# Another order of all five engines' work in the turns of a gated delta rule kernel

## The reference, cut to what matters

```python
q, k = l2norm(conv(q)) * 64 ** -0.5, l2norm(conv(k))      # causal convolutions of 4 taps; v = conv(v)
def step(S, xs):
    q_t, k_t, v_t, g_t, b_t = xs
    S = S * exp(g_t)
    kv = k_t @ S
    delta = (v_t - kv) * b_t
    S = S + outer(k_t, delta)
    return S, q_t @ S
o = o * rsqrt(mean(o * o) + EPS) * norm_weight * sigmoid(z)
return o.reshape(B, S, 2048) @ w_out.T
```

## Time and profile before

| | |
|---|---|
| median of 3 runs (lowest, highest) | 3103.07 us (3101.98, 3112.64) |
| the profiled execution, its own time | 3102.21 us |
| its span, first to last instruction | 3100.4 us |
| mean granted clock of TensorE in it | 0.98 |
| TensorE's instructions | 42816 matmuls, 42816 weight loads |
| busy share: PE, DVE, ACT, POOL | 93%, 79%, 57%, 36% |

### The profile page before, as it was taken

How to read it: one execution, slowest core, us unless ns; L and a number is a source line. 1 busy time by engine, 2 the same in 40 slices (tenths; PEclk the granted TensorE clock), 3 DMA queues, 4 the chain that set the end, 5 groups by cost and what they waited for, 6 DMA issues and landing times. The chain is left out here.

```text
span 3100.4 us, 101425 instructions
## 1 busy us (share of the span) xinstructions
PE 2889.3 (93%) x42816; PEld 1955.3 (63%) x42816; DVE 2436.7 (79%) x5610; ACT 1753.3 (57%) x3242; POOL 1103.5 (36%) x904
## 2 busy tenths in 40 slices
PE   6699999999999999999999999999999999789998
PEld 3366666666666666666666666666666666645555
DVE  7688888888887888888888888888788888645654
ACT  6456666666665655666666566656566666333432
POOL 1444444334444444444434344444444444100000
PEclk9899999999999999999999999999999999899999
DMA  5455555454545444554555545544454545300000
GB/s 154 80 85 97 83 83 84 75 97 82 84 81 98 79 79 78 98 84 77 83 97 84 82 78 101 84 80 78 73 103 74 82 83 83 76 17 25 28 21 14
DMA packets 1298099, 241.85 MB, mean 78 GB/s; under 512 B 1248240, under 2 KB 1269104, under 8 KB 1296496
## 3 DMA queue, kind: packets, MB, share of 16 engines
q1 hardware_dynamic: 1297648, 235.36, 44.0%
HBM read 120.13 MB, written 39.58 MB: 52 GB/s over the span
## 5 line engine op out<-in xcount | busy, mean ns | idle before, releaser
L1342 PE MATMUL bank<-xT,w_sb 128*128 128x512 f32 x2048 | 980.5, 612 | 9.7 <-PEq L516 5.2
L784 POOL TENSOR_TENSOR kq<-kq,product 128x510 f32<-128x510 f32 (+2 forms) x384 | 449.2, 1183 | 717.4 <-ACT kq L873 707.4
L1342 PEld LDWEIGHTS bank<-xT,w_sb 128*128 128x128 f32 x2048 | 372.5, 192 | 374.5 <-issue 346.9
L772 POOL TENSOR_TENSOR dec_ap<-gcrow,gcb 128x1024 f32<-128x1024 f32 x64 | 121.9, 1904 | 653.7 <-DMA gcb<-gcb_d 653.7
L1088 DVE SCALAR_TENSOR_TENSOR kq<-bank,cw,kq 128x510 f32<-128x510 f32 (+2 forms) x384 | 285.8, 745 | 54.8 <-ACT kq L873 45.2
L1088 DVE SCALAR_TENSOR_TENSOR v_c<-bank,cw,v_c 128x510 f32<-128x510 f32 (+2 forms) x384 | 285.8, 744 | 15.9 <-ACT v_c L873 6.9
L1353 PE MATMUL bank<-kq 64*64 64x128 f32 x4096 | 277.6, 273 | 20.3 <-POOL kq L784 8.3
L940 ACT COPY delta<-bank 128x256 f32<-128x256 f32 x256 | 95.3, 372 | 343.7 <-PE bank L1410 343.5
L1457 PE MATMUL bank<-wo,u_sq 128*128 128x256 f32 x1024 | 260.5, 398 | 4.2 <-DVE u_sq L1180 3.5
L879 ACT ACTIVATE product<-bank,cw 128x512 f32<-128x512 f32 x384 | 249.2, 684 | 6.8 <-PE bank L1342 2.8
L1147 DVE TENSOR_TENSOR ap_mat<-bank,dec_ap 128x512 f32<-128x512 f32 x256 | 160.1, 684 | 115.9 <-PE bank L1435 108.9
(11 more groups left out here) (168 smaller groups left out, 5456.1 us busy)
## 6 DMA issues: line engine op xcount, KB each, us to landing
xT<-xT_d SPq DMA_DIRECT2D x64, 512.0 KB, 4.0
gcrow<-gcrow_d SPq DMA_DIRECT2D x128, 256.0 KB, 4.5
k_r<-k_tok SPq DMA_DIRECT2D x512, 64.0 KB, 2.3
v_r<-k_tok SPq DMA_DIRECT2D x512, 64.0 KB
a_d<-ap_mat SPq DMA_DIRECT2D x256, 64.0 KB
z_t<-z_d SPq DMA_DIRECT2D x256, 64.0 KB, 2.5
w_sb<-in_w_qkvz SPq DMA_DIRECT2D x8, 1024.0 KB, 6.8
x_un<-eye_un SPq DMA_DIRECT2D x64, 128.0 KB, 3.9
```

Source lines behind the costliest of these rows:

```text
L784: nc.gpsimd.tensor_tensor(t[:, :, d:SEQ], t[:, :, d:SEQ], prod[:, :, 0:SEQ - d], ALU.add).then_inc(tap_added[i], 1)
L1342: ins = nc.tensor.matmul(bank[:, :], w_two[m.grp % 2][:, h, s * P:(s + 1) * P], xT[:, h, :], start=(h == 0), stop=(h == HT - 1))
```

## The change

The order of work within a turn is changed on all engines; no product, transfer or vector instruction is added or removed. Some banks of the ring change their place with it, and so do the waits that protect them. Below are the turns as they are after it, shortened: lines with + are placed anew, the others are kept from the kernel before, whose own order is printed above. Indents are shortened. New semaphores: `mag_done`, `score_full[0]`, `tap_prod[3]` and `[4]`, `mats_done[1]` and `[2]`; gone: `acc_done`, `mats_done[0]`.

SyncE (only the step numbers fall by one; the order of the transfers stays):

```diff
...
 if s[4]:
+    wait_for(sp, mats_done[3], s[4], 1)
+    units_out(s[4])
...
+if s[3]:
+    wait_for(sp, kx_done[1], s[3], 1)
+    k_turned(s[3])
 if s[4]:
+    wait_for(sp, zt_done, s[4], 1)
+    z_out(s[4])
+    x_out(s[4])
...
```

GpSimd:

```diff
...
+if s[5]:
+    wait_for(pool, tap_added[0], s[5], 1)
+    add_tap(s[5], 0, 2)
+    wait_for(pool, tap_prod[3], s[5], 1)
+    add_tap(s[5], 1, 1)
...
+    wait_for(pool, tap_prod[5], s[5], 1)
+    add_tap(s[5], 1, 3)
+    wait_for(pool, cols_done, s[5], 1)
+    scale_decays(s[5])
+    wait_for(pool, egrow_done, s[5], 1)
+    end_decays(s[5])
+    clamp(s[5], 1)
...
+    scale_q(s[5], 1)
+    scale_q(s[5], 0)
 if s[4]:
+    wait_for(pool, gc_in, s[4], 48)
+    differences(s[4])
+    wait_for(pool, z_exp[0], s[4], 1)
+    clamp(s[4], 0)
     wait_for(pool, decay_done, s[4], 1)
     mask(s[4])
+    add_tap(s[4], 0, 1)
```

ScalarE:

```diff
...
 if s[4]:
     wait_for(act, comb_done[1], s[4], 1)
     gates(s[4], 1)
+if s[1]:
+    wait_for(act, proj_full[1], s[1], 1)
+    first_tap(s[1], 1, ring(s[1], 0))
 if s[4]:
     wait_for(act, comb_done[0], s[4], 1)
     gates(s[4], 0)
+if s[3]:
+    wait_for(act, zoff_full, s[3], 1)
+    outer_out(s[3])
+if s[2]:
+    log_z(s[2], 0)
...
+if s[3]:
+    wait_for(act, zr_full[0], s[3], 1)
+    delta_out(s[3], 0)
+    square_q(s[3])
...
     wait_for(act, diff_done, s[1], 1)
     magnitudes(s[1])
...
+    wait_for(act, proj_full[6], s[1], 1)
+    wait_for(act, z_log[0], s[1], 1, back=1)
+    exp_z(s[1], 0, ring(s[1], 1))
 if s[3]:
     wait_for(act, zr_full[1], s[3], 1)
     delta_out(s[3], 1)
 if s[2]:
     wait_for(act, sub_done[14], s[2], 1)
     turn_units(s[2])
 if s[1]:
+    wait_for(act, mag_done, s[1], 1)
+    decays(s[1])
+    wait_for(act, proj_full[5], s[1], 1)
+    first_tap(s[1], 5, ring(s[1], 1))
+    wait_for(act, proj_full[7], s[1], 1)
+    exp_z(s[1], 1, ring(s[1], 2))
+    first_tap(s[1], 3, ring(s[1], 3))
+    tap_product(s[1], 1, 1, ring(s[1], 3))
+    wait_for(act, tap_added[0], s[1], 1)
+    tap_product(s[1], 1, 2, ring(s[1], 3))
...
+if s[3]:
+    wait_for(act, zr_full[2], s[3], 1)
+    delta_out(s[3], 2)
...
+    wait_for(act, k_f_in, s[1], 128)
+    squares(s[1])
+    wait_for(act, tap_added[1], s[1], 1)
+    tap_product(s[1], 1, 3, ring(s[1], 3))
     wait_for(act, proj_full[4], s[1], 1)
     first_tap(s[1], 4, ring(s[1], 0))
     wait_for(act, sumk_done, s[1], 1)
     norms(s[1])
+    row_decays(s[1])
...
 if s[3]:
+    wait_for(act, zr_full[3], s[3], 1)
+    delta_out(s[3], 3)
     wait_for(act, o_full[3], s[3], 1)
     square_o(s[3], 1)
     square_o(s[3], 0)
     outer16_out(s[2])
 if s[3]:
     wait_for(act, ss_full[1], s[3], 1)
+    log_var(s[3], 1, ring(s[3], 0))
+    wait_for(act, ss_full[0], s[3], 1)
+    log_var(s[3], 0, ring(s[3], 3))
 if s[0]:
     wait_for(act, proj_full[0], s[0], 1)
+    first_tap(s[0], 0, ring(s[0], 3))
 if s[2]:
     wait_for(act, p1_full, s[2], 1)
     inner_out(s[2])
+if s[1]:
+    wait_for(act, z_clamped[1], s[1], 1)
+    wait_for(act, comb_done[1], s[1], 1, back=2)
+    log_z(s[1], 1)
...
```

VectorE:

```diff
...
 if s[2]:
+    sub_rest(s[2], 10)
+    sub_product(s[2], 11)
...
+    sub_product(s[2], 14)
+    sub_rest(s[2], 14)
 if s[1]:
     wait_for(dve, gc_in, s[1], 48)
     tail(s[1])
+if s[4]:
+    wait_for(dve, op_full[0], s[4], 1)
+    accumulate(s[4], 0, ring(s[4], 2))
+if s[3]:
+    decay_state(s[3], 1)
...
+if s[3]:
+    wait_for(dve, st_full[1], s[3], 1)
+    wait_for(dve, sdec_done[1], s[3], 1)
+    new_state(s[3], 1)
+    wait_for(dve, ks_full[2], s[3], 1)
+    residual(s[3], 2)
+if s[1]:
+    wait_for(dve, tap_done[5], s[1], 1)
+    conv(s[1], 5, ring(s[1], 1))
...
+if s[3]:
+    wait_for(dve, st_full[2], s[3], 1)
+    wait_for(dve, sdec_done[2], s[3], 1)
+    new_state(s[3], 2)
+    wait_for(dve, ks_full[3], s[3], 1)
+    residual(s[3], 3)
+if s[1]:
+    wait_for(dve, rk_done, s[1], 1)
+    wait_for(dve, rhs_done[3], s[1], 1, back=2)
+    columns(s[1])
+    conv(s[1], 4, ring(s[1], 0))
+    wait_for(dve, score_full[0], s[1], 1)
+    wait_for(dve, deca_done, s[1], 1)
+    wait_for(dve, o_full[3], s[1], 1, back=2)
+    matrices(s[1], 0, ring(s[1], 3))
+    wait_for(dve, score_full[1], s[1], 1)
+    matrices(s[1], 1, ring(s[1], 1))
+    wait_for(dve, score_full[2], s[1], 1)
+    matrices(s[1], 2, ring(s[1], 2))
+    wait_for(dve, score_full[3], s[1], 1)
+    matrices(s[1], 3, ring(s[1], 0))
+    turn_v(s[1], 1)
+if s[3]:
+    wait_for(dve, usq_done[1], s[3], 1)
+    add_squares(s[3], 1)
+    wait_for(dve, usq_done[0], s[3], 1)
+    add_squares(s[3], 0)
+if s[1]:
+    turn_v(s[1], 0)
+if s[2]:
+    wait_for(dve, z16_done, s[2], 1)
+    turn_back(s[2])
+if s[1]:
+    scale_k(s[1])
+if s[3]:
+    wait_for(dve, var_log[1], s[3], 1)
+    combine(s[3], 1, ring(s[3], 0))
+if s[0]:
+    wait_for(dve, tap_done[0], s[0], 1)
+    conv(s[0], 0, ring(s[0], 3))
+if s[3]:
+    wait_for(dve, var_log[0], s[3], 1)
+    combine(s[3], 0, ring(s[3], 3))
+    wait_for(dve, gate_done[1], s[3], 1)
+    gated(s[3], 1)
+    wait_for(dve, gate_done[0], s[3], 1)
+    gated(s[3], 0)
+if s[1]:
+    wait_for(dve, x_un_in, s[1], 16)
+    wait_for(dve, a_un_in, s[1], 16)
+    sub_product(s[1], 0)
+    sub_rest(s[1], 0)
+    sub_product(s[1], 1)
+if s[0]:
+    wait_for(dve, tap_done[1], s[0], 1)
+    conv(s[0], 1, ring(s[0], 0))
+if s[1]:
+    sub_rest(s[1], 1)
+    sub_product(s[1], 2)
+    sub_rest(s[1], 2)
+    sub_product(s[1], 3)
+    sub_rest(s[1], 3)
+if s[2]:
+    wait_for(dve, st_full[0], s[2], 1)
+    new_state(s[2], 0)
+if s[1]:
+    sub_product(s[1], 4)
+    sub_rest(s[1], 4)
+    sub_product(s[1], 5)
+    sub_rest(s[1], 5)
+if s[0]:
+    wait_for(dve, conv_done[0], s[0], 1)
+    wait_for(dve, v_f_in, s[0], 128, back=1)
+    turn_k(s[0], 0)
+if s[1]:
+    sub_product(s[1], 6)
+if s[0]:
+    wait_for(dve, conv_done[1], s[0], 1)
+    turn_k(s[0], 1)
+if s[1]:
+    sub_rest(s[1], 6)
+    sub_product(s[1], 7)
+    sub_rest(s[1], 7)
+    sub_product(s[1], 8)
+    sub_rest(s[1], 8)
+if s[2]:
+    wait_for(dve, ks_full[1], s[2], 1)
+    residual(s[2], 1)
+if s[1]:
+    sub_product(s[1], 9)
+    sub_rest(s[1], 9)
+    sub_product(s[1], 10)
...
```

TensorE:

```diff
...
+if s[3]:
+    wait_for(pe, qg_done[0], s[3], 1)
+    wait_for(pe, og_done[0], s[3], 1, back=1)
+    output(s[3], 0)
+    wait_for(pe, state_done[0], s[3], 1)
+    key_state(s[3], 1)
+if s[1]:
+    wait_for(pe, conv_done[0], s[1], 1)
+    project(s[1], 3, ring(s[1], 3))
+    wait_for(pe, z_exp[0], s[1], 1)
+    project(s[1], 5, ring(s[1], 1))
+if s[4]:
+    wait_for(pe, og_done[0], s[4], 1)
+    project_out(s[4], 0, ring(s[4], 2))
+if s[3]:
+    wait_for(pe, rhs_done[1], s[3], 1)
+    solve(s[3], 1)
+if s[1]:
+    project(s[1], 7, ring(s[1], 2))
+if s[3]:
+    wait_for(pe, delta_done[1], s[3], 1)
+    advance(s[3], 1)
+    output(s[3], 1)
+    wait_for(pe, state_done[1], s[3], 1)
+    key_state(s[3], 2)
+if s[4]:
+    wait_for(pe, z_exp[1], s[4], 1, back=-3)
+    project_out(s[4], 1, ring(s[4], 0))
+if s[3]:
+    wait_for(pe, rhs_done[2], s[3], 1)
+    solve(s[3], 2)
+if s[1]:
+    wait_for(pe, conv_done[1], s[1], 1)
+    project(s[1], 4, ring(s[1], 0))
+if s[3]:
+    wait_for(pe, delta_done[2], s[3], 1)
+    advance(s[3], 2)
+    output(s[3], 2)
 if s[2]:
+    wait_for(pe, z_in, s[2], 64)
+    join16_inner(s[2])
+if s[3]:
+    wait_for(pe, state_done[2], s[3], 1)
+    key_state(s[3], 3)
+if s[1]:
+    wait_for(pe, tap_added[2], s[1], 1)
+    wait_for(pe, tap_prod[5], s[1], 1)
+    scores(s[1], 0, ring(s[1], 3))
+    wait_for(pe, conv_done[5], s[1], 1)
+    scores(s[1], 1, ring(s[1], 1))
+if s[3]:
+    wait_for(pe, rhs_done[3], s[3], 1)
+    solve(s[3], 3)
+if s[1]:
+    wait_for(pe, tap_added[5], s[1], 1)
+    scores(s[1], 2, ring(s[1], 2))
+if s[3]:
+    wait_for(pe, delta_done[3], s[3], 1)
+    output(s[3], 3)
+if s[1]:
+    wait_for(pe, conv_done[4], s[1], 1)
+    scores(s[1], 3, ring(s[1], 0))
 if s[2]:
+    wait_for(pe, p16_done, s[2], 1)
+    wait_for(pe, x_row_in, s[2], 64)
+    join16_outer(s[2])
+if s[0]:
+    wait_for(pe, x_T_in, s[0], 16)
+    wait_for(pe, mats_done[1], s[0], 1, back=1)
+    project(s[0], 0, ring(s[0], 3))
+if s[3]:
+    wait_for(pe, sq_added[1], s[3], 1)
+    sum_squares(s[3], 1, ring(s[3], 0))
+    wait_for(pe, sq_added[0], s[3], 1)
+    sum_squares(s[3], 0, ring(s[3], 3))
 if s[2]:
+    wait_for(pe, z16_done, s[2], 1)
+    join_inner(s[2])
+if s[0]:
+    wait_for(pe, mats_done[2], s[0], 1, back=1)
+    project(s[0], 1, ring(s[0], 0))
 if s[2]:
+    wait_for(pe, p1_done, s[2], 1)
+    wait_for(pe, xtop_done, s[2], 1)
+    join_outer(s[2])
+if s[0]:
+    wait_for(pe, mats_done[3], s[0], 1, back=1)
+    wait_for(pe, comb_done[1], s[0], 1, back=3)
+    project(s[0], 2, ring(s[0], 2))
 if s[2]:
+    wait_for(pe, zoff_done, s[2], 1)
+    solve(s[2], 0)
+if s[0]:
+    project(s[0], 6, ring(s[0], 1))
 if s[2]:
+    wait_for(pe, delta_done[0], s[2], 1)
+    advance(s[2], 0)
```

(83 more changed lines are left out.)

308 lines of the change are left out of this document (53 added, 255 removed).

## The result

| | before | after |
|---|---|---|
| median of the runs beside each other | 3105.28 us (3101.98 to 3112.64, 4 runs) | 3189.79 us (3186.88 to 3192.09, 4 runs) |
| profiled execution: own time, span | 3102.21, 3100.4 us | 3189.55, 3187.7 us |

The kernel became slower: ratio 1.0277, 95% interval 1.0247 to 1.0307, 85 us. The direction was forecast; the size, 3127 us with a range to 3185, was not.

A forecast was written before the change was run, and what follows sets the result against it. It took the scores-to-joins round trip and TensorE's work as equal bounds, 38.1 us; after, the trip's 40.1 plus 0.5 of stops, clock and jitter gives 40.6 a turn against 40.2, times 63: 25 us more, 3127 us (range 3065 to 3185).

The forecast's parts named there:

- fetch term: TensorE's stops for bringing in instructions fall to 0.65 us a turn against 1.0, 22 us less in all.
- legs of the round trip: Parts of the way from one step's scores to its joins and scores again: 40.1 us a turn against 38.1 before.
- The columns: VectorE's triangular columns, first to last, with `conv(1)` among them: 12.15 us against 10.96 before.
- VectorE's wait on `a_un`: VectorE's first column would wait for the transfer of `a_un`, up from almost none.
- Smaller new waits, inside that idle time: TensorE: `solve(0)` waits 0.3 us, `key_state(1)` 0.5 us for `new_state(0)`, within the 2.0 us it idles each turn.
- wrong if the z_t waits stay rare: Sign against the forecast: TensorE's z_t waits should rise from 10.6 us to some 60 or more, in most turns.
- Step 2 of the prediction: VectorE's column 0 waits for `a_un` until 11.3 us; `conv(1)`, columns, `new_state(0)` and TensorE's `key_state(1)` queue behind.
- clock term: Most half-clock stretches on TensorE begin right after a stop; a third fewer saves 7 us.
- The end of the pipeline: Filling and draining the pipeline: depth unchanged, within 8 us either way, taken as 0.
- The rival "much slower": `z_out` queues behind `k_turned`, 1 us more on the trip, `a_un` lands at 11.8: 41.5 us a turn, 3184 us; chance 0.11.

The follow-up runs named there:

- `differences` small: Changed kernel with GpSimd's `differences` cut to 4 of the 64 columns of each group, nothing moved: 3111.14 us, ratio 1.0038.
- `conv(1)` first: Changed kernel with `conv(1)` moved ahead of `sub_product(0)` on VectorE: 3101.57 us, ratio 0.9998.
- state behind `conv(1)`: Changed kernel with `new_state(0)` moved directly behind `conv(1)` on VectorE: 3153.78 us, ratio 1.0175.

## Why the prediction was right in direction, and wrong in size and in its reason

**The fetch term held.** Forecast: 22 us of stops less; measured in the turns: 61 to 30, 31 us less, mostly gone from `join16_outer` (25.8 to 7.5) and new at `key_state` (5.1) as said; at `scores` they stayed (6.9 and 6.1).

**The legs of the round trip held too, but one.** From the rows above and the same turn's others: `scores(3)` to `conv(0)` 1411.04 to 1417.65, 6.6 (6.8 forecast); to the first product 1422.35, 11.3 (11.3); the columns to 1435.08, 12.7 (12.15); to the join at 1444.39, 9.3 (9.75); to the end of `scores(3)` at 1451.41, 7.0 (6.9). Sum 40.4 against 40.1. These legs go once round, from `scores(3)` to `scores(3)`, so their sum is the length of this turn whatever binds it. What shows that the trip does not is in the fourth: z_t had landed at 1443.74, 0.65 us before TensorE came to the join. The trip alone is 39.7 us, under the 40.1 forecast. The columns are the one leg that was too cheap: their first products were priced from a turn in which `differences` had ended before them, and one took 1.2 us more. (That turn had two instructions stalled under `add_tap`, some 0.6 us, which the 10.96 us holds without saying so.) VectorE's wait on `a_un` came as forecast, 42.8 us in 55 turns.

**The step that failed is "Smaller new waits, inside that idle time".** It priced `key_state(1)`'s wait at 0.5 us a turn and counted it as covered by idle time that the z round trip would leave. Measured: 98.8/60 = 1.6 us, and no such idle time: with the join later, z_t waits vanish and the time stays (3184.53). By the prediction's own sign, "wrong if the z_t waits stay rare", its reason failed: 6.7 us in 10 turns. That it forecast a slower kernel all the same is in part luck, since what it priced is not what made the kernel slower. As the trace reads, the loop that binds runs from `key_state(1)` through the chunks to VectorE's `residual(3)`, columns, matrices, gates and first triangular columns, and back to `new_state(0)`; the runs test its last part, from the first columns on, and not the rest. Step 2 of the prediction named this queue ("and with it `key_state(1)` on TensorE"), and did not follow it round. Why it is 1.1 us longer than counted is the second half of the error: nothing in the prediction asked what GpSimd does while VectorE's products run, though the diff moves `conv(1)` from one side of them to the other. With `differences` small, some 74 us of the loss go; that is shown. That it is VectorE's operand reads that are held is the explanation, and the runs show its timing only.

**The clock term had the wrong sign.** I took 7 us off since fewer stops would mean fewer stretches. The stretches went from 40.9 to 64.8 us: eleven of sixteen start within 1.5 us of the end of a wait of 1.9 to 2.8 us for the state. They follow TensorE's idle gaps, whoever makes them, and more the long ones than their sum: in `conv(1)` first, with 14.5 us of that wait, none over 0.4 us, 10.2 us are left at half clock (200 to 2640 us), and in state behind `conv(1)`, with 80 us of waits for states, none over 1.5 us, nothing is.

**The end of the pipeline,** taken as 0 within 8 us, cost 9: from the last `t_un` to the end of the span 439.3 us against 429.5, with `t_un` 1 us earlier at the start. The drain has 34 us at half clock against 17.

The sum put right: 40.6 to 41.47 us is 0.87 x 63 = 55 us, the ends 9: 3127 + 64 = 3191, against 3189.8. The 41.47 is measured, so this says where the time went and does not derive it. The rival "much slower" gave 3184, near by accident: it lengthened the z trip by `z_out` behind `k_turned`, and that trip did not bind. Its 41.5 us also leaves out the half microsecond of stops, clock and jitter that the forecast adds to the trip.

## What to carry to other kernels

When an order changes, write down for each engine which instructions will newly run at the same time as those of another engine, not only who waits for whom: VectorE products of 0.2 us became 1.4 to 1.9 us and the profile shows no wait for it, only a longer instruction; comparing the shortest and longest of one form finds them, in the trace of the kernel before already. Put VectorE work that reads a bank beside GpSimd's long instructions, and its work on two SBUF tensors beside GpSimd's pauses; and if a transfer is brought forward or back, look again which of the two it moves. When two loops are nearly equal, follow both to their start before counting one as the other's cover.
